# Selective scans of layer 0: channels of one state, or 4 states x 32 channels, on the partitions

## What is computed

```
delta = softplus(dts + bias)                      # dts from a rank-12 projection
h     = exp(delta * A[d, n]) * h + (delta * u) * B[n]
y     = sum over n of h * C[n]
out   = sum over directions of (y + D * u), directions 2 and 3 reversed
```

## Time and profile before

| | |
|---|---|
| median of 3 runs | 27879.47 us (27868.37 to 27930.98) |
| profiled execution | 27921.66 us, its span 27919.9 us |
| scans of layer 0 ("s0") | from 1097 to 19959 us of the span, 256 units |
| busy share of the span | PE 89%, DVE 91%, ACT 64%, POOL 84% |
| DMA | 4583 MB, mean 164 GB/s |

### The profile page before, as it was taken

How to read it: one execution, slowest core, us unless ns; L and a number is a source line. 1 busy time by engine, 2 the same in 40 slices (tenths; PEclk the granted TensorE clock), 3 DMA queues, 4 the chain that set the end, 5 groups by cost and what they waited for, 6 DMA issues and landing times. The chain is left out here.

```text
span 27919.9 us, 261599 instructions
## 1 busy us (share of the span) xinstructions
PE 24874.1 (89%) x70946; PEld 10612.0 (38%) x70946; DVE 25291.2 (91%) x22482; ACT 17866.2 (64%) x30091; POOL 23560.1 (84%) x10168
## 2 busy tenths in 40 slices
PE   8788988998888899889888888988889988888888
PEld 3333443443443344344344434434334433333332
DVE  8899999999999999999999999999851189999996
ACT  2477777777777777777777777777423266666662
POOL 1599999999999999999999999999502189999994
PEclk9999999999999999999999999999999999999999
DMA  5533333333333343333333333333543277777778
GB/s 202 193 140 148 150 140 145 147 142 141 151 143 142 145 152 138 145 150 144 140 149 149 138 147 149 141 143 150 178 133 109 79 232 230 229 229 230 230 230 293
DMA packets 1194275, 4583.10 MB, mean 164 GB/s; under 512 B 254368, under 2 KB 292272, under 8 KB 827472
## 3 DMA queue, kind: packets, MB, share of 16 engines
q1 hardware_dynamic: 1093568, 4217.15, 42.5%
q10 hardware_dynamic: 99248, 349.22, 3.4%
HBM read 3907.28 MB, written 658.64 MB: 164 GB/s over the span
## 5 line engine op out<-in xcount | busy, mean ns | idle before, releaser
L1049 DVE TENSOR_TENSOR_SCAN s_h<-s_dA,s_state,s_dbu 128x512 f32<-128x512 f32 x12236 | 14960.7, 1269 | 59.2 <-ACT s_dA L884 50.7
L971 POOL TENSOR_TENSOR s_dbu<-s_du,s_b_sb 128x1536 f32<-128x1536 f32 (+1 forms) x4610 | 14188.6, 3084 | 430.9 <-DMA s_b_sb<-rows 428.7
L884 ACT ACTIVATE s_dA<-s_delta,s_negA 128x512 f32<-128x512 f32 x12288 | 8289.9, 685 | 5515.3 <-DVE s_h L1049 5501.6
L711 PE MATMUL s_y_ps<-s_hc,s_ident 128*128 128x512 f32 x17920 | 8785.2, 602 | 1.5 <-DVE s_hc L1059 1.5
L983 POOL TENSOR_TENSOR s_hc_pool<-s_h,s_c_sb 128x512 f32<-128x512 f32 (+1 forms) x4864 | 7843.8, 1617 | 575.4 <-DVE s_h L1049 514.6
L721 PE MATMUL s_y_ps<-s_hc_pool,s_ident 128*128 128x512 f32 x12800 | 6379.7, 600 | 105.2 <-ACT s_yo L846 105.2
L1059 DVE TENSOR_TENSOR s_hc<-s_h,s_c_ps 128x1024 f32<-128x1024 f32 (+1 forms) x5632 | 5526.0, 981 | 169.5 <-issue 140.9
L711 PEld LDWEIGHTS s_y_ps<-s_hc,s_ident 128*128 128x128 f32 x17920 | 3491.1, 195 | 2162.5 <-issue 1932.4
L1049 DVE TENSOR_TENSOR_SCAN s_h<-s_dA_sb,s_state,s_dA 128x512 f32<-128x512 f32 x3060 | 3816.0, 1266 | 295.1 <-PE s_dA L672 290.8
L701 PE MATMUL s_c_ps<-s_bc,s_sel 96*128 96x512 bf16 x6400 | 2369.0, 390 | 1455.2 <-DVE s_hc L1059 1441.2
L721 PEld LDWEIGHTS s_y_ps<-s_hc_pool,s_ident 128*128 128x128 f32 x12800 | 2379.7, 193 | 2786.9 <-issue 2532.9
(11 more groups left out here) (175 smaller groups left out, 17734.1 us busy)
## 6 DMA issues: line engine op xcount, KB each, us to landing
s_b_sb<-rows SPq DMA_DIRECT2D x1794, 1024.0 KB, 6.8
s_c_sb<-rows SPq DMA_DIRECT2D x1216, 1024.0 KB, 5.2
s_u<-U SPq DMA_DIRECT2D x257, 768.0 KB
Y<-s_yo ACTq DMA_DIRECT2D x256, 768.0 KB, 3.8
s_prev<-Y SPq DMA_DIRECT2D x128, 768.0 KB, 4.4
s_u<-U SPq DMA_DIRECT2D x193, 256.0 KB
U<-f_row SPq DMA_DIRECT2D x24, 2048.0 KB, 17.3
U<-f_col SPq DMA_DIRECT2D x24, 2048.0 KB, 7.1
```

Of the source, the lines that this page charges most:

```text
L711: last = pe.matmul(y_ps[:, t, :], ident[:, :], hc[:, s % 2, j, :], start=begins(g, s), stop=nd > 1 and s == NS - 1)
L884: act.activation(place, delta[g % 2][:, t, :], ACT.Exp, scale=negA[g % 2][:, a:a + 1]).then_inc(dA_ready, 1)
L971: pool.tensor_tensor(dbu[:, i % AHEAD, :, :], a, b, ALU.mult).then_inc(dbu_ready, 1)
L1049: dve.tensor_tensor_scan(h[:, s % (2 * GROUP), j, :], decay, given, initial, ALU.mult, ALU.add).then_inc(scanned, 1)
```

## The change

A function of its own, `packed_scans`, takes the place of `scan_phase` for "s0". It has the same 256 units of 48 tiles of 128 x 512, but a tile holds 4 states x 32 channels. A unit is 12 steps n (4 groups of 4 states by 3 blocks of 128 channels) of 4 tiles i (32 channels each).

- All inputs are turned. du is transposed once per unit; scaled by the 16 rows of B with positions on the partitions, in instructions of 384 elements on ACT (nine states, 36 instructions) or 1536 elements on POOL (six states) and DVE (one state); PE turns all 48 tiles back (192 transposes) into PSUM, `x_ps`, a ring of 3. POOL's products du * B with spread B are gone.
- The decay's delta is spread over the four states by a way through DRAM: one store of delta, 12 loads. Decays go to SBUF, a ring of 8.
- C is spread over the partitions by 4 DMAs per unit into SBUF. The matmuls that spread C, the bf16 split and its takes are gone.
- Products by C: DVE takes tile 0 of the 4 (12 a unit), POOL the other 3 in one instruction of 1536 elements (12 a unit), and POOL also copies the states for the next chunk, which ACT did.
- The sum over states is 4 matmuls a step, one for each tile, with a stationary operand `fold` of 128 x 32, each writing 32 of the 128 partitions of y.
- DVE's order in a step is scans 0, 1, 2, product of the same step, scan 3. PE's order is the turn of tile 0 of the next step, the sum of the step before last, then the turns of tiles 1 to 3. The ring `hc` of products has two slots.

```diff
@@ after layer0_features @@
+def packed_scans(nc, U, Y, rows_dram, delta_dram, w_x, w_dt, w_bias, w_logs, w_D, ident_in, fold_in):
...
+    NG, NJ, NI, R = 4, ND0, 4, 4
+    STEPS, QB = NG * NJ, T // 128
+    TILES = STEPS * NI
+    units = B * K0 * NCHUNK
+    BACK = K0 // 2 * NCHUNK
+    ROWS_BC = 2 * N_STATE
+    DECAYS, INPUTS, H_RING, REP = 8, 4, 3, 4
+    BY_ACT = ((0, 1), (0, 1), (0, 1, 2), (0, 1))
+    BY_DVE = ((3,), (), (), ())
+    BY_POOL = ((2,), (2, 3), (3,), (2, 3))
+    OWN = 1
+    on_pe = dict(xproj=0, rows=1, dt=(2, 3, 3), turn_du=(7, 8, 8))
+    on_act = dict(take=0, rows=1, dt=(2, 3, 3), soft=4, turn_du=(7, 8, 8), evacuate=(0, 1, 2), store=3)
+    on_pool = dict(du=5)
+    SCALE_ACT = {0: (1, 0), 1: (1, 1), 3: (2, 0), 4: (2, 1), 6: (3, 0), 7: (3, 1), 9: (4, 0), 10: (4, 1)}
+    SCALE_DVE = {10: 4}
+    SCALE_POOL = {0: (1, 0), 1: (1, 1), 3: (2, 0), 6: (3, 0), 7: (3, 1), 9: (4, 0)}
...
+        u = [sb(f"u{q}", [128, NJ, T]) for q in range(2)]
+        delta_rep = sb("delta_rep", [128, REP, NI, T])
+        duT, rowsT = sb("duT", [128, QB, NJ * NI, 32]), [sb(f"rowsT{q}", [128, QB, N_STATE]) for q in range(2)]
+        scaled = sb("scaled", [128, 2, QB, NJ * NI, R, 32])
+        c_sb = [sb(f"c_sb{q}", [128, NG, T]) for q in range(2)]
+        dA = sb("dA", [128, DECAYS, T])
+        h, hc = sb("h", [128, H_RING, NI, T]), sb("hc", [128, 2, NI, T])
...
+        x_ps = pb("x_ps", [128, INPUTS, T])
+        y_ps = pb("y_ps", [128, NJ, T])
+        prep_ps = pb("prep_ps", [128, T])
...
+            def turn_input(n, i):
+                tile, x = n * NI + i, n // NJ
+                if n % NJ == 0 and i == 0:
+                    pe.wait_ge(scaled_act, QB * scaled_to(BY_ACT, x + 1))
+                    pe.wait_ge(scaled_dve, scaled_to(BY_DVE, x + 1))
+                    pe.wait_ge(scaled_pool, scaled_to(BY_POOL, x + 1))
+                wait(pe, scanned, tile - INPUTS + 1)
+                for b in range(QB):
+                    last = pe.transpose(x_ps[:, tile % INPUTS, b * 128:(b + 1) * 128],
+                                        scaled[:, x % 2, b, n % NJ * NI + i, :, :].rearrange("p r c -> p (r c)"), ident[:, :])
+                last.then_inc(input_turned, 1)
+            def direct(g, t):
+                wait(pe, evacuated, (g - 1) * NJ + t + 1)
+                if opens(g):
+                    last = pe.matmul(y_ps[:, t, :], D_ident[:, t, :], u[g % 2][:, t, :], start=True, stop=False)
+                    if t == NJ - 1:
+                        last.then_inc(direct_done, 1)
+                if folds(g):
+                    pe.wait_ge(prev_in, 16 * (fold_of(g) + 1))
+                    last = pe.matmul(y_ps[:, t, :], ident[:, :], prev[:, t, ::-1], start=True, stop=False)
+                    if t == NJ - 1:
+                        last.then_inc(prev_summed, 1)
+            def state_sum(n):
+                g, m = divmod(n, STEPS)
+                if m < NJ:
+                    direct(g, m)
+                pe.wait_ge(hc_ready, n + 1)
+                pe.wait_ge(own_ready, n + 1)
+                for i in range(NI):
+                    last = pe.matmul(y_ps[32 * i:32 * i + 32, m % NJ, :], fold[:, :], hc[:, n % 2, i, :],
+                                     start=m < NJ and not opens(g) and not folds(g), stop=m >= STEPS - NJ)
+                last.then_inc(summed, 1)
+            def unit(g):
+                more = g + 1 < units
+                for m in range(STEPS):
+                    n = g * STEPS + m
+                    ahead = n + 1 < units * STEPS
+                    if ahead:
+                        turn_input(n + 1, 0)
+                    if n >= 2:
+                        state_sum(n - 2)
+                    if ahead:
+                        turn_input(n + 1, 1)
+                    if more and m == on_pe["xproj"]:
+                        xproj(g + 1)
+                    if more and m == on_pe["rows"]:
+                        turn_rows(g + 1)
+                    if more:
+                        for t in range(NJ):
+                            if on_pe["dt"][t] == m:
+                                dt(g + 1, t)
+                    if ahead:
+                        turn_input(n + 1, 2)
+                    if more:
+                        for t in range(NJ):
+                            if on_pe["turn_du"][t] == m:
+                                turn_du(g + 1, t)
+                    if ahead:
+                        turn_input(n + 1, 3)
...
+            def scale(x, part):
+                g = x // NG
+                if part == 0:
+                    act.wait_ge(rows_taken, g + 1)
+                    act.wait_ge(du_taken, (g + 1) * NJ)
+                    wait(act, input_turned, (x - 1) * NJ * NI)
+                for b in range(part * QB // 2, (part + 1) * QB // 2):
+                    for r in BY_ACT[x % NG]:
+                        s = x % NG * R + r
+                        act.activation(scaled[:, x % 2, b, :, r, :], duT[:, b, :, :], ACT.Copy,
+                                       scale=rowsT[g % 2][:, b, s:s + 1]).then_inc(scaled_act, 1)
...
+                wait(act, scanned, tile - DECAYS + 1)
+                a = m * NI + i
+                act.activation(dA[:, tile % DECAYS, :], delta_rep[:, x % REP, i, :], ACT.Exp,
+                               scale=negA[:, direction(g), a:a + 1]).then_inc(dA_ready, 1)
...
+            def scale(x, part):
+                g = x // NG
+                if part == 0:
+                    pool.wait_ge(rows_taken, g + 1)
+                    pool.wait_ge(du_taken, (g + 1) * NJ)
+                    wait(pool, input_turned, (x - 1) * NJ * NI)
+                r = BY_POOL[x % NG][part]
+                s = x % NG * R + r
+                pool.tensor_tensor(scaled_slot(x, r), duT[:, :, :, :],
+                                   rowsT[g % 2][:, :, s:s + 1].unsqueeze(3).broadcast_to([128, QB, NJ * NI, 32]),
+                                   ALU.mult).then_inc(scaled_pool, 1)
+            def times_c(n):
+                g, m = divmod(n, STEPS)
+                pool.wait_ge(scanned, (n + 1) * NI)
+                if goes_on(g):
+                    pool.tensor_copy(state[:, m * NI:(m + 1) * NI], h[:, n % H_RING, :, T - 1]).then_inc(state_saved, 1)
+                if m == 0:
+                    pool.wait_ge(c_in[g % 2], 16 * R * (g // 2 + 1))
+                wait(pool, summed, n - 1)
+                c = c_sb[g % 2][:, m // NJ:m // NJ + 1, :].broadcast_to([128, NI - OWN, T])
+                pool.tensor_tensor(hc[:, n % 2, OWN:NI, :], h[:, n % H_RING, OWN:NI, :], c, ALU.mult).then_inc(hc_ready, 1)
...
+            def scan(n, i):
+                g, m = divmod(n, STEPS)
+                tile = n * NI + i
+                if i == 0:
+                    wait(dve, hc_ready, n - H_RING + 1)
+                    wait(dve, own_ready, n - H_RING + 1)
+                    wait(dve, state_saved, saves_to(n - H_RING + 1) if n >= H_RING else 0)
+                dve.wait_ge(dA_ready, tile + 1)
+                dve.wait_ge(input_turned, tile + 1)
+                a = m * NI + i
+                initial = state[:, a:a + 1] if continues(g) else 0.0
+                dve.tensor_tensor_scan(h[:, n % H_RING, i, :], dA[:, tile % DECAYS, :], x_ps[:, tile % INPUTS, :],
+                                       initial, ALU.mult, ALU.add).then_inc(scanned, 1)
+            def times_c(n):
+                g, m = divmod(n, STEPS)
+                dve.wait_ge(scanned, n * NI + OWN)
+                if m == 0:
+                    dve.wait_ge(c_in[g % 2], 16 * R * (g // 2 + 1))
+                wait(dve, summed, n - 1)
+                c = c_sb[g % 2][:, m // NJ:m // NJ + 1, :].broadcast_to([128, OWN, T])
+                dve.tensor_tensor(hc[:, n % 2, 0:OWN, :], h[:, n % H_RING, 0:OWN, :], c, ALU.mult).then_inc(own_ready, 1)
+            scale(0)
+            for g in range(units):
+                for m in range(STEPS):
+                    for i in range(NI):
+                        scan(g * STEPS + m, i)
+                        if i == 2:
+                            times_c(g * STEPS + m)
+                        if i == 1 and m in SCALE_DVE and (SCALE_DVE[m] < NG or g + 1 < units):
+                            scale(g * NG + SCALE_DVE[m])
...
-    scan_phase(nc, "s0", (B, K0, ND0, 1, R0), U0, Y0, rows0, arg["a_xproj"], arg["a_dt"], arg["a_small"],
-               arg["a_D"], arg["keep"], arg["ident"], arg["select"])
+    packed_scans(nc, U0, Y0, rows0, scratch("delta0", (2, 128, ND0, T)), arg["a_xproj"], arg["a_dt"], arg["a_bias"],
+                 arg["a_logs"], arg["a_D"], arg["ident"], arg["fold"])
...
+    fold = np.tile(np.eye(32, dtype=f), (4, 1))
...
```

310 lines of the change are left out of this document (306 added, 4 removed).

## The result

The changed kernel takes 31355.43 us (median of 4 runs, 31343 to 31377) against 27878.91 (27868 to 27931): ratio 1.1244, 95% interval 1.1224 to 1.1263. It is 12.4% slower, 3476 us. The prediction said 37200, range 33500 to 41000: right in sign, far too high, outside the range.

What follows compares the result with a forecast made beforehand. DVE's product waiting in every step for PE's sum was taken to bound the kernel: 100.8 + 2.1 + 1.9 + 3.5 + 1.7 = 110.0 us per unit against 73.7, giving 37200 us; eight-in-ten range 33500 to 41000.

Steps and rivals of the forecast that it cites:

- What bounds the phase afterwards: Work sums alone gave 65 to 72 us per unit; the hand-written orders were to set a slower pace.
- DVE's work, 65.3 per unit: DVE's 48 scans 56.6, 12 products 7.0 and one scaling 1.64: 65.3 us per unit, 5.9 less than before.
- POOL's state copies: Twelve copies of states per unit on POOL, taken at 0.15 us each (bounds 0 and 1.23), 1.8 us.
- The chain per step, 8.40 us: Two scans, PE's wake, turn, sum, DVE's start, product and last scan in series: 8.40 us, 100.8 for twelve steps.
- The sum: PE's eight MATMULs per step, assumed one after another at 0.43 each: 3.44 us, lower bound 0.86.
- Two scans ahead of the turn: PE's turn of the next step's tile 0 waits for scan 1, through a ring of three: 2.45 us.
- Direct matmuls, burst: Direct matmuls ahead of sums, +1.9 us per unit; ACT's projection takes, scalings, decays and softplus delaying PE's turn, +3.5.
- The port: DVE's product, with both operands in SBUF, waits while POOL works there: +2.1 us per unit; DVE's scaling nothing.
- The clock: One fall of PE to half clock per unit after a long wait: +1.7 us per unit.
- rival 3: PE's clock falls more often: every second step 39400 us, nearly every step 41500, always half clock 47000; chance 0.16.
- rival 1: The sum's four column groups overlap and DVE's product waits for POOL at the port instead: 35400 or 33800 us; chance 0.28.
- rival 2: Groups overlap and POOL's tensor_tensor does not lock the port: 29500 or 32600 us, one after another 36700; chance 0.09.

Runs made afterwards that it cites:

- the fastest: Changed kernel with sum before turn, three slots, C in PSUM copied ahead of decays, early third-group scaling, DVE's scaling on ACT, product behind fourth scan: 27034.8 us.
- the kernel with both inputs: Changed kernel with an `x_ps` ring of three instead of four and sums writing all 128 partitions one after another: 39500.6 us.

## Why the prediction was wrong, by its steps

- **What bounds the phase afterwards**: right in kind. Work per engine (65 to 72 us) does not give the time; the orders do. DVE waits for the sum, POOL for scans (5063 us before its state copies), and no engine is full.
- **DVE's work, 65.3 per unit**: right; scans at 1.18, no waits of their own. **POOL's state copies**, 0.15 taken of 0 to 1.23: 0.14 to 0.16 from start to start. POOL's products 3.40; most of its scalings 3.15 from start to start, where 3.40 was taken.
- **The chain per step, 8.40 us**: the step that failed. Two of its six terms were wrong. *The sum*: 3.44 from matmuls of 128 columns of weights, measured 1.00. It was bounded (0.86 to 3.44) and the wrong end was chosen; the choice was worth 4908 us. *Two scans ahead of the turn*: this was no unknown of the chip but the ring's size read wrongly in the code, three for four; one scan (1.18 us) too many, worth 2981 us. With both set right, the same chain gives 1.27 + 0.06 + 0.49 + 1.06 + 0.04 = 2.92 us, and the product is due at 3.55: at full clock there is **no** wait, and that is what more than four steps in ten show. The chain was to set the pace of every step; of the waits that the changed kernel has, 9.1 of 13.2 us per unit stand behind late scalings instead. Built with the wrong inputs, the step is 8.48 in a quarter of the steps and over 10 in most others.
- **Direct matmuls, burst**: right in kind, too small. The burst was priced at 3.5 (5 without cover); it makes 5.7 of the waits, and its removal gave 3.6 of time and 5.5 of waits. A second wait of this kind, that of step 2 for the scaling of the next group (2.6 with the direct matmul and the half clock behind it), was in no term. What was priced as an addition to the chain is the larger part of the waits in the kernel as it is.
- **The port**: right in mechanism, too small for the kernel that was measured. Priced at 2.1 with long steps, it takes 6.6 in products and 1.9 in the scaling, which was put at nothing because it was thought to lie beside the sum. It grows as the steps shorten: whatever lets DVE run sooner lets it meet POOL more often.
- **The clock**: too small in the kernel that was forecast (2300 us between 37200 and 39501, by its long steps). In the measured one the phase is at 0.80 where 1.7 us per unit was set. Sums at half clock cost 1.86 for 1.00 and turn a chain of 2.9 us into one of over 4 with a wait. What it costs by itself no run isolates; the waits fall and the clock rises together (0.852 over the whole changed kernel, 0.892 with the sum first, 0.939 in the fastest), and cause and effect run both ways there. The sign set for rival 3, a clock under 0.9, came as well. The last price of rival 3, half clock always, fell.
- **Rivals**: the time lies between rival 1 (33800 with all groups side by side) and rival 2 (29500 without the port). Rival 1's picture, groups side by side and the port taking over, is the one seen; it too had the ring of three. Its seven steps of 8.8 are not there: 780 of 3071 steps take 6.6 to 6.9 us and 650 take 8.0 to 8.7. The rule of the Trainium skill (TensorEngine Tiling (Array Packing), Key Properties), that column tiles operate independently, is what the trace shows: 1.00 us. I had a rule and no row against a price from rows of another form, and gave the rule 0.28.
- **The range** failed because all the cases that it was made from had the ring of three. That the sign is right is no proof of the chain: it is right although the wait forecast for every step is missing in four of ten. The ends of the unknown cost were in it, the misreading was in none.

## What to carry to other kernels

Before a chain is priced, every ring on it is to be read off the code with its line and put into the working: a slot more or less shifts the whole chain by an instruction of another engine (here a scan of 1.18 us). The wait of an in-order engine is to be followed one instruction further back: the sum was late because the turn ahead of it was, and the turn mostly because ACT's scaling was. If both operands of a product on DVE lie in SBUF while GpSimd works there, part of the time gained on DVE is given back, here until one operand lay in PSUM. And where an operand's copy is urgent, its place in the helper engine's queue counts: moving one copy ahead of four decays gave 704 us, moving one scaling a step forward 925.

## What the runs showed of the hardware that was not expected

- Eight fp32 MATMULs of 512 columns with 32 columns of weights in four column groups take 1.00 us from the first start to the next instruction at full clock, 1.86 at half; eight of 128 columns of weights take 3.44 (12036.61 to 12040.05 in the kernel with both inputs). That is a quarter of the time and a little more: the four groups start 0.007 us apart, and the second MATMUL of each 0.45 us behind its first.
- POOL's product of 1536 elements keeps a DVE product of two SBUF operands waiting for its whole length (3.94 us for 0.55 of work), but does not slow the product with one operand in PSUM (0.676 us on average) nor the scans (1.18 to 1.20 from start to start).
- PE's turns ran at half clock behind its waits of 4.37 and 4.56 us in the changed kernel, but also behind shorter ones: in the kernel with both inputs, behind waits of 1.61, 0.52 and 0.61 us, a turn takes 0.88 us to the next start instead of 0.49 and the sum 4.68 instead of 3.44. In steps with little waiting turns and sums ran at full clock, though transposes are more than half of PE's busy time (7784 of 13660 us from 1200 to 19000 in the fastest kernel): 0.92 was granted in its phase.

```profile
1097.00:19066.00 17969.00, 13787.80 (x82004) 7189.21 (x82004) 16329.95 (x15358) 15737.59 (x27107) 15946.17 (x7549) 0.92 0.38 100
```
